# Writing out the last slots of a recurrent layer by hand, and moving three steps around its start

## The reference, cut to what matters

```python
# end of layer 2
h = _layer_norm(x, ln_mlp_scale, ln_mlp_offset)
x = x + jax.nn.gelu(h @ w_fc1 + b_fc1, approximate=False) @ w_fc2 + b_fc2
# layer 3
xa = _ln(x, ln1_w, ln1_b)
sx = jnp.concatenate([state[:, 1:2] - xa[:, :1], xa[:, :-1] - xa[:, 1:]], axis=1)
xxx = jnp.tanh((xa + sx * maa_x) @ maa_w1).reshape(b, l, 5, DM)
xxx = jnp.einsum('blfd,fde->blfe', xxx, maa_w2)
xm = xa[:, :, None] + sx[:, :, None] * (maa_stack + xxx)
xk, xw, xv, xr, xg = (xm[:, :, j] for j in range(5))
w = jnp.exp(-jnp.exp(time_decay + jnp.tanh(xw @ td_w1) @ td_w2))
r, k, v, g = xr @ Wr.T, xk @ Wk.T, xv @ Wv.T, _silu(xg @ Wg.T)
def step(s, rkvw):
    r_t, k_t, v_t, w_t = rkvw
    a = k_t[..., :, None] * v_t[..., None, :]
    out = jnp.einsum('bhi,bhij->bhj', r_t, u * a + s)
    return a + w_t[..., :, None] * s, out
# out, normed per head -> og
x1 = x + og * g @ Wo.T
xc = _ln(x1, ln2_w, ln2_b)
sx2 = jnp.concatenate([state[:, 0:1] - xc[:, :1], xc[:, :-1] - xc[:, 1:]], axis=1)
rr = jax.nn.sigmoid((xc + sx2 * ffn_maa_r) @ Wfr.T)
kk = jnp.square(jax.nn.relu((xc + sx2 * ffn_maa_k) @ Wfk.T))
return x1 + rr * (kk @ Wfv.T)
```

## Time and profile before

| | |
|---|---|
| median of 3 timed runs | 1012.68 us |
| the three runs | 1005.13, 1012.68, 1013.59 us |
| the profiled execution: its time | 1015.81 us |
| the profiled execution: its span | 1014.0 us |
| PE busy | 956.1 us (94% of the span) |
| DVE, ACT, POOL busy | 596.8, 451.3, 411.4 us |
| mean granted clock of TensorE | 0.983 of 2.4 GHz |

### The profile page before, as it was taken

The page is one execution under the profiler, slowest core; times in us unless marked ns, Lnnn a source line. Parts: engine busy times, 40 slices in busy tenths (PEclk is TensorE's granted clock), DMA queues, the critical chain, the costliest instruction groups (busy, mean ns, idle before and its releaser), DMA issues.

```text
span 1014.0 us, 21415 instructions
## 1 busy us (share of the span) xinstructions
PE 956.1 (94%) x8312; PEld 802.4 (79%) x8312; DVE 596.8 (59%) x972; ACT 451.3 (45%) x990; POOL 411.4 (41%) x572
## 2 busy tenths in 40 slices
PE   6999998988999999999999999999997999999986
PEld 4777776866789888899988998888996876778754
DVE  5999994767534444334464344443357648999851
ACT  3566763248543333333344333333323244666543
POOL 2243356875366234334156342343317722443320
PEclk9999999999999999999999999999999997999978
DMA  8100000310021111011101111110100100000000
GB/s 293 32 22 2 2 1 22 112 53 2 1 69 38 47 52 52 22 50 36 54 17 53 40 49 47 52 52 21 42 27 11 43 1 1 2 7 6 13 6 16
DMA packets 24146, 37.13 MB, mean 37 GB/s; under 512 B 4432, under 2 KB 16528, under 8 KB 23824
## 3 DMA queue, kind: packets, MB, share of 16 engines
q1 hardware_dynamic: 24080, 36.23, 11.4%
HBM read 35.17 MB, written 1.05 MB: 36 GB/s over the span
## 4 chain that ended last, share of the span: by engine, by line
PE 71%; DVE 14%; issue 5%; ACT 5%; POOL 4%; DMA 1%; DVEq 0%; ACTq 0%; POOLq 0%; SPq 0%
PE ps L1252 17%; PE ps L757 12%; PE ps L1269 9%; PE ps L1905 6%; PE ps L1311 6%; PE ps L1287 3%; PE ps L855 3%; DVE sb L634 2%; PE ps L1297 2%; DVE sb L628 2%; PE ps L2058 1%; PE ps L1983 1%; DVE sb L2350 1%; ACT sb L1692 1%; PE ps L269 1%
## 5 line engine op out<-in xcount | busy, mean ns | idle before, releaser
L804 POOL TENSOR_TENSOR sb<-sb 128x256 fp32r<-128x256 f32 (+1 forms) x128 | 101.4, 792 | 286.0 <-DMA sb<-in_heads_a 151.5
L1252 PE MATMUL ps<-sb 128*128 128x512 f32 x768 | 187.8, 396 | 1.0 <-issue 1.0
L1252 PEld LDWEIGHTS ps<-sb 128*128 128x128 f32 x768 | 139.5, 188 | 33.0 <-ACT sb L1385 3.1
L757 PE MATMUL ps<-sb 128*128 128x256 f32 x1152 | 149.0, 286 | 1.2 <-DVE sb L901 1.1
L757 PEld LDWEIGHTS ps<-sb 128*128 128x128 f32 x1152 | 141.4, 191 | 4.5 <-issue 2.6
L806 POOL TENSOR_TENSOR sb<-sb 128x256 fp32r<-128x256 f32 (+1 forms) x128 | 116.7, 912 | 10.1
L1482 DVE SCALAR_TENSOR_TENSOR sb<-ps,sb 128x512 fp32r<-128x512 f32 x64 | 45.1, 746 | 96.3 <-ACT sb L1418 96.3
L1269 PE MATMUL ps<-sb 128*128 128x256 f32 x768 | 99.2, 285 | 0.4 <-DVE sb L1450 0.4
L1269 PEld LDWEIGHTS ps<-sb 128*128 128x128 f32 x768 | 95.0, 191 | 3.0 <-issue 0.9
L1462 DVE TENSOR_REDUCE sb<-ps 128x8 f32<-128x520 f32 x32 | 22.4, 700 | 126.6 <-PE ps L1287 126.6
L1905 PE MATMUL ps<-sb 128*128 128x128 f32 (+2 forms) x576 | 87.7, 308 | 9.3 <-ACT sb L2208 6.4
(11 more groups left out here) (215 smaller groups left out, 1660.5 us busy)
## 6 DMA issues: line engine op xcount, KB each, us to landing
sb<-in_heads_a SPq DMA_DIRECT2D x32, 386.0 KB, 3.0
sb<-in_heads_c SPq DMA_DIRECT2D x16, 256.0 KB, 3.7
sb<-in_heads_b SPq DMA_DIRECT2D x32, 128.0 KB, 3.0
sb<-in_mlp_a SPq DMA_DIRECT2D x16, 128.5 KB, 2.1
sb<-in_mlp_b SPq DMA_DIRECT2D x16, 128.0 KB, 2.0
sb<-in_w_r SPq DMA_DIRECT2D x1, 2048.0 KB, 7.6
sb<-in_encT SPq DMA_DIRECT2D x1, 1024.0 KB, 7.3
sb<-in_ctx SPq DMA_DIRECT2D x1, 1024.0 KB, 7.1
```

The costliest lines, as they stand in the source:

```text
L757: last = pe.matmul(m.acc(t), lhsT[x], rhs[w], start=opens and n == 0, stop=False, skip_group_check=True)
L804: pool.tensor_tensor(high, src, one, ALU.mult).then_inc(*G.did(name + "_high", u))
L1252: last = pe.matmul(m.ps[u][:, c, :], m.w_parts[u][w][:, (KD * q + k) * P:(KD * q + k + 1) * P], rows[x][:, k, c * 512:(c + 1) * 512], star ...
```

## The change

`add_row_gpsimd` for `b_fc2` goes behind the splits of round 1. On PE, `fc1` of the last block (second half, round 3) goes ahead of the first tile's `turn`; on DVE, the split of its result goes from ahead of slot 0 into slot 3, behind tile 0's `shift` and `lora_rows`. In slot 5 on DVE, `gate` goes ahead of `receive`; on PE, two `warm` matmuls go ahead of the wait for that gate. PE's and ACT's loops end after slot 8 and DVE's after slot 11; what was left of tiles 3 to 7 is written out step by step. In it the keys and the receptance of tiles 5 and 7 (`APART`) get PSUM banks of their own, `ffn1` is cut in two (`ffn_keys`, with a signal of its own, and `ffn_receive`), `ffn2` of tiles 5 and 7 no longer waits for the receptance, three groups of `warm(m.td_ps, 3)` are added, and a one-column activation, `table`, fetches the ACT table at a chosen place. ACT's `receive` gets a wait for `rf` of the tile before.

```diff
@@ -1868,6 +1866,8 @@
+LAST = TILES - 1
+APART = (LAST - 2, LAST)
@@ -1987,8 +1987,8 @@
-        if i == 3:
-            warm(m.ps[0][:, 0, :], 4)
+        if i in (1, 3):
+            warm(m.ps[0][:, 0, :], i + 1)
@@ -2038,40 +2038,49 @@
-        if i >= 1:
-            pe.wait_ge(*done["rf"].at(i - 1))
+        if i == APART[0]:
+            pe.wait_ge(*done["mixed"].at(LAST))
+        elif i >= 1:
+            pe.wait_ge(*done["rf"].at(i - 2 if i > APART[0] else i - 1))
         for k in range(KD):
-            last = pe.transpose(m.c1[:, k * P:(k + 1) * P], m.xn_last[i % 2][:, k * P:(k + 1) * P], m.ident[:, :])
+            last = pe.transpose(m.key_bank(i)[:, k * P:(k + 1) * P], m.xn_last[i % 2][:, k * P:(k + 1) * P], m.ident[:, :])
...
-    @of_tile
-    def ffn1(i):
+    ffn_parts = [(m.wr[:, W_FK, :, :], m.wr[:, W_FR, :, :], k, 1) for k in range(KD)]\
+        + [(m.wfks, m.wfrs, k, 0) for k in range(KD)]
+    @of_tile
+    def ffn_keys(i):
...
-        parts = [(m.wr[:, W_FK, :, :], m.wr[:, W_FR, :, :], k, 1) for k in range(KD)]\
-            + [(m.wfks, m.wfrs, k, 0) for k in range(KD)]
         for e in range(KD):
-            product(m.c1[:, e * P:(e + 1) * P], [(wk[:, k, e * P:(e + 1) * P], m.xc[:, k, :, s:s + S])
-                                                 for wk, _, k, s in parts])
-        for n, (_, wr, k, s) in enumerate(parts):
+            last = product(m.key_bank(i)[:, e * P:(e + 1) * P],
+                           [(wk[:, k, e * P:(e + 1) * P], m.xc[:, k, :, s:s + S]) for wk, _, k, s in ffn_parts])
+        last.then_inc(*done["kk_raw"].did(i))
+    @of_tile
+    def ffn_receive(i):
+        for n, (_, wr, k, s) in enumerate(ffn_parts):
             for b in range(2):
-                last = pe.matmul(m.c1[b * S:(b + 1) * S, D:2 * D], m.xc[:, k, b, s:s + S], wr[:, k, :], start=n == 0,
-                                 stop=n == len(parts) - 1)
+                last = pe.matmul(m.receive_bank(i)[b * S:(b + 1) * S, D:2 * D], m.xc[:, k, b, s:s + S], wr[:, k, :],
+                                 start=n == 0, stop=n == len(ffn_parts) - 1)
...
-        pe.wait_ge(*done["rr"].at(i))
-        product(m.c1[:, 0:D], [(m.kk[:, k * P:(k + 1) * P], m.wr[:, W_FV, k, :]) for k in range(KD)])\
+        if i not in APART:
+            pe.wait_ge(*done["rr"].at(i))
+        product(m.key_bank(i)[:, 0:D], [(m.kk[:, k * P:(k + 1) * P], m.wr[:, W_FV, k, :]) for k in range(KD)])\
...
-    fc1(pe, ph, m, rows_split, 0, 1, 3)
-    for slot in range(TILE_SLOTS):
+    for u in range(STREAMS):
+        fc1(pe, ph, m, rows_split, u, 1, 3)
+    for slot in range(LAST + 2):
@@ -2079,13 +2088,13 @@
-            fc1(pe, ph, m, rows_split, 1, 1, 3)
...
-        ffn1(slot - 5)
+        ffn_keys(slot - 5)
+        ffn_receive(slot - 5)
@@ -2101,6 +2110,34 @@
+    gather(LAST - 1)
+    decay2(LAST)
+    spread1(LAST)
+    center(LAST - 1)
+    ffn_keys(LAST - 3)
+    ffn_receive(LAST - 3)
+    turn_ffn(LAST - 2)
+    turn_heads(LAST - 1)
+    ffn2(LAST - 3)
+    warm(m.td_ps, 3)
+    attended(LAST - 1)
+    ffn_keys(LAST - 2)
+    gather(LAST)
+    warm(m.td_ps, 3)
+    center(LAST)
+    turn_ffn(LAST - 1)
+    ffn_receive(LAST - 2)
+    turn_heads(LAST)
+    ffn2(LAST - 2)
+    warm(m.td_ps, 3)
+    attended(LAST)
+    ffn_keys(LAST - 1)
+    ffn_receive(LAST - 1)
+    turn_ffn(LAST)
+    ffn2(LAST - 1)
+    ffn_keys(LAST)
+    ffn_receive(LAST)
+    ffn2(LAST)
@@ -2188,24 +2225,30 @@
         for k in range(KD):
-            last = act.activation(m.xc[:, k, :, 1:S + 1], m.c1[:, k * P:(k + 1) * P].rearrange("p (b s) -> p b s", b=2),
-                                  ACT.Identity, bias=m.col("r2_b", k), scale=m.col("r2_w", k))
+            last = act.activation(m.xc[:, k, :, 1:S + 1],
+                                  m.key_bank(i)[:, k * P:(k + 1) * P].rearrange("p (b s) -> p b s", b=2), ACT.Identity, bias=m.col("r2_b", k), scale=m.col("r2_w", k))
...
     def relu(i):
-        act.wait_ge(*done["kk_rr"].at(i))
-        act.activation(m.kr[:, :], m.c1[:, 0:D], ACT.Relu).then_inc(*m.own_act.did("relu", i))
+        act.wait_ge(*done["kk_raw" if i in APART else "kk_rr"].at(i))
+        act.activation(m.kr[:, :], m.key_bank(i)[:, 0:D], ACT.Relu).then_inc(*m.own_act.did("relu", i))
...
-        act.activation(m.thf[:, :], m.c1[:, D:2 * D], ACT.Tanh, scale=0.5).then_inc(*done["rr"].did(i))
+        if i >= 1:
+            act.wait_ge(*done["rf"].at(i - 1))
+        act.activation(m.thf[:, :], m.receive_bank(i)[:, D:2 * D], ACT.Tanh, scale=0.5).then_inc(*done["rr"].did(i))
...
+    def table(function):
+        act.activation(m.th[:, 0:1], m.col("eps"), function)
@@ -2272,6 +2315,42 @@
+    heads(LAST - 2)
+    gate(LAST)
+    project(LAST)
+    decay1(LAST)
+    ffn_rows(LAST - 3)
+    f_stats(LAST - 2)
+    decay2(LAST)
+    f_normed(LAST - 2)
+    square(LAST - 1)
+    std(LAST - 1)
+    table(ACT.Tanh)
+    relu(LAST - 3)
+    relu_square(LAST - 3)
+    heads(LAST - 1)
+    ffn_rows(LAST - 2)
+    receive(LAST - 3)
+    f_stats(LAST - 1)
+    relu(LAST - 2)
+    relu_square(LAST - 2)
+    f_normed(LAST - 1)
+    table(ACT.Sqrt)
+    square(LAST)
+    std(LAST)
+    table(ACT.Tanh)
+    heads(LAST)
+    ffn_rows(LAST - 1)
+    receive(LAST - 2)
+    f_stats(LAST)
+    f_normed(LAST)
+    relu(LAST - 1)
+    receive(LAST - 1)
+    relu_square(LAST - 1)
+    ffn_rows(LAST)
+    relu(LAST)
+    relu_square(LAST)
+    receive(LAST)
@@ -2425,10 +2504,9 @@
-    for r in (2, 3):
-        for u in range(STREAMS):
-            mlp_split(vec, ph, m, u, 1, r)
-    for slot in range(TILE_SLOTS):
+    for u, r in ((0, 2), (1, 2), (0, 3)):
+        mlp_split(vec, ph, m, u, 1, r)
+    for slot in range(LAST + 5):
@@ -2440,16 +2518,43 @@
+        if slot == 3:
+            mlp_split(vec, ph, m, 1, 1, 3)
...
+        if slot == 5:
+            gate(slot - 4)
...
-        gate(slot - 4)
+        if slot != 5:
+            gate(slot - 4)
...
+    products0(LAST)
+    bonus(LAST - 1)
+    out_heads(LAST - 1)
+    products1(LAST)
+    group_sum(LAST - 1)
+    scan0(LAST)
+    group_rstd(LAST - 1)
+    group_norm(LAST - 1)
+    scan1(LAST)
+    attended(LAST - 1)
+    receive(LAST)
+    ffn(LAST - 3)
+    close(LAST - 3)
+    bonus(LAST)
+    out_heads(LAST)
+    group_sum(LAST)
+    group_rstd(LAST)
+    group_norm(LAST)
+    attended(LAST)
+    for i in (LAST - 2, LAST - 1, LAST):
+        ffn(i)
+        close(i)
@@ -2684,6 +2789,8 @@
+        m.key_bank = lambda i: m.ps[1][:, 0, :] if i in APART else m.c1
+        m.receive_bank = lambda i: m.ps[1][:, 1, :] if i in APART else m.c1
@@ -2717,6 +2824,7 @@
+        m.tile_done["kk_raw"] = Signal(m.done["ctx_ps"].sem, len(ITEMS))
@@ -2810,8 +2918,11 @@
+            for sem, value in free[3]["wv"]:
+                pool.wait_ge(sem, value)
+            mlp_gpsimd(pool, ph["mlp2"], m, 20, (1,), False)
...
-            mlp_gpsimd(pool, ph["mlp2"], m, 20, False, free[3]["wv"])
+            mlp_gpsimd(pool, ph["mlp2"], m, 20, (2, 3), False)
```

More of the change, by code:

```diff
@@ L911, in mlp_vector, with mlp_gpsimd @@
             context_norm_vector(vec, m, r)
-def mlp_gpsimd(pool, ph, m, loads, first, before):
-    for sem, value in before:
-        pool.wait_ge(sem, value)
-    for r in range(1, MLP_ROUNDS):
+def mlp_gpsimd(pool, ph, m, loads, rounds, first):
+    for r in rounds:
         split_fc1(pool, ph, m, loads, r)
@@ L2410, in ffn @@
             vec.wait_ge(*done["out"].at(i - 1))
-        vec.scalar_tensor_tensor(out=m.rf[:, :], in0=m.thf[:, :], scalar=1.0, in1=m.c1[:, 0:D], op0=ALU.add,
+        vec.scalar_tensor_tensor(out=m.rf[:, :], in0=m.thf[:, :], scalar=1.0, in1=m.key_bank(i)[:, 0:D], op0=ALU.add,
                                  op1=ALU.mult).then_inc(*done["rf"].did(i))
@@ L2793, in _ @@
             attn0_gpsimd(pool, ph["mlp0"], m)
-            mlp_gpsimd(pool, ph["mlp0"], m, 0, True, [])
+            mlp_gpsimd(pool, ph["mlp0"], m, 0, range(1, MLP_ROUNDS), True)
             inorm_gpsimd(pool, heads[1], m, free[1])
```

## The result

The changed kernel takes 997.46 us in the median (995.07 to 1000.22), the kernel before took 1011.45 (1005.13 to 1013.59, one execution more than stood above); the ratio is 0.9867, with an interval of 0.9828 to 0.9906, so that the change makes the kernel 0.9 to 1.7% faster. The profiled execution took 1000.22 us with a span of 998.4, against 1015.81 and 1014.0. So 14.0 us went in the median and 15.6 in the profile, where 19.6 had been forecast.

A forecast was written before the change was run, and what follows sets the result against it. PE was taken to bound most of the kernel, with clock falls behind its waits and tile 7's hand-overs at the end. 1.1 + 5.5 + 13.0 + 0 = 19.6 us off 1012.68 gave 993.1 us, range 988 to 999.

The forecast's parts named there:

- the signs named as right: Clock 1.00 at tile 1's gate, prompt gate, earlier lora, POOL waits moved, tile 7's x1 some 11 us before the last store.
- the signs named as wrong: Long half clock in either place, PE idle behind a table load, MLP 2 us sooner, or tile 7's x1 barely sooner.
- The bias row, 0 us: In the last MLP, moving the row leaves POOL's sum unchanged, so PE's wait only shifts; 0, bounds 2.3 gained, 1 lost.
- Rival 3: In the last MLP, the bias row's move pays in full; 990.8 us, chance 0.04.
- The start, 1.1 us: Ahead of tile 0, moving the last block's fc1 and split brings lora 1.1 us sooner; bounds 0 and 1.5.
- The gate, 5.5 us: At tile 1's gate, removing PE's wait and the clock fall gains 5.5 us, carried on; bounds 1.9 and 6.8.
- rival 2: At tile 1's gate, the clock still falls, giving 1.9 instead of 5.5 us; 996.7 us, chance 0.11.
- The end, 13.0 us: In the written-out last tiles, the new order gains 14.4 us, taken as 13.0; bounds 8.5 and 14.4.
- the half fall that was allowed for: At PE's wait ahead of tile 4's ffn2, a short clock fall costing about 2.5 us, put at one half.
- Rival 1: At PE's wait for tile 4's receptance, clock low to about 984; end gives 8.5, total 997.6 us, chance 0.14.
- rival 4: At ACT's table loads in the end, drains take 2.8 us more; 995.9 us, chance 0.03.
- Rival 5: The written-out end runs at half clock throughout, losing 8.6 us there; 1014.7 us, chance 0.04.

The follow-up runs named there:

- undo_row: The changed kernel with the bias row ahead of round 1's splits on POOL again; 996.9 us, 0.986 of the time before.
- row_late: The changed kernel with the bias row behind the split of the last fc1 weights on POOL; 998.8 us (of 3), 0.984 of the time before.
- no_tables: The changed kernel without the three one-column activations that fetch ACT tables early; 999.9 us, 0.988 of the time before.
- undo_gate: The changed kernel with tile 1's gate behind receive on DVE again, without the two warm matmuls ahead of it; 1000.8 us, 0.989 of the time before.
- banks_only: The changed kernel with loops to slot 16 in the old order, keeping own PSUM banks and shorter waits; 1002.4 us, 0.989 of the time before.
- no_warm: The changed kernel without the nine warm matmuls of the written-out end; 995.7 us, 0.982 of the time before.
- undo_start: The changed kernel with the last block's fc1 behind tile 0's turn and its split ahead of slot 0 again; 1000.5 us, 0.989 of the time before.
- recv_first: The changed kernel with ACT's tanh of tile 4's receptance ahead of heads and ffn_rows; 997.9 us, 0.984 of the time before.
- undo_end: The changed kernel with loops to slot 16 again, without written-out end, own banks, table fetches or warm matmuls there; 1010.1 us, 0.997 of the time before.
- gate_both: The changed kernel with tile 2's gate ahead of receive too and three warm matmuls ahead of it; 994.3 us, 0.980 of the time before.

## Why the prediction was right, and where it was off

The time lies inside the range and the direction is as forecast; the value was 4.4 us too low. In the profile 4.0 us are missing, and two misses are in them: the gate brought 5.4 us less than its term and the end 1.4 us more. That the second hid a part of the first is luck. Of the signs named as right all came (clock, gate, `lora`, waits for POOL, though with an MLP 0.7 us longer, `x1` of tile 7 11.0 us ahead of the end of the last `close`), and of the signs named as wrong none came at the two places named; the long fall stood at a third place that no sign watched.

- *The bias row, 0 us:* right, and by its reason, that POOL's sum of work holds PE. It measured -0.7 in the profile. What the sum did not have is that the wait in the middle can bring a short fall of the clock, which is most of it. Rival 3 is refuted by `undo_row`, and `row_late` shows what it takes: the row has to leave the sum ahead of the last `fc1` split.
- *The start, 1.1 us:* 1.6 in its place (10.35 to 8.74 us), less the 0.6 by which the MLP ends later, is about the 1.1 of the profile at tile 0's `mix1`.
- *The gate, 5.5 us:* tile 3's `mix1` came 6.4 us sooner, 5.3 beyond the start's 1.1. The chain of DVE steps that was followed through the slot was right to 0.2 us. The step that failed is the next sentence, "it is carried on". DVE without waits means that PE has them: in a slot where DVE is the bound, PE waited 1.10 us for the next gate, and a fall of the clock took 5.2 us back (119.8 us in the middle against 114.6 in `undo_row` and `no_tables`, where the same wait was followed by none). Nothing of the 5.5 was carried on in the profiled execution. The text looked for falls where PE had waited in the old profile, and rival 2 put the fall at the same gate, not at the one behind. Its time, 996.7, is near what came. By the mean clocks two of the four executions had the fall, so the median holds about half of that loss; only one of them was profiled.
- *The end, 13.0 us:* 14.4 in the profile, which is the sum of the steps to 0.1 us, without the half fall that was allowed for. `x1` of tile 6 was put at 975.8 on the old clock and came 6.08 + 0.42 us behind tile 6's norm, 975.7; `x1` of tile 7 at 986.4, 986.45 measured; the end at 997.5, 997.5 measured. That `ffn2` of tile 4 would win nothing was right (2.10 us of waiting, 2.12 before), and so was the price if the clock falls there, in kind: 1.5 us (`undo_gate`, `undo_row`), not 2.5. Rival 1's long fall was in no version with the new order. What the text had wrong is the share: it gave the order all of it, and `banks_only` shows that the banks and their shorter waits carry 7.7 of the 14.3.
- *Table loads:* rival 4 did not come. A tanh is 0.02 us behind its load of 1.28 in the version without fetches, so that the drain that the Trainium skill (ScalarE: Activation LUTs, "What ACT_TABLE_LOAD costs") adds, about 1.38 us, is not seen, neither as idle time on either side of the load (in the changed kernel ACT ends at 965.43, loads from 965.45 to 966.73 and goes on at 966.75) nor in the end of 28.3 us.
- *Rival 5,* half clock throughout, was in no version with the new order.
- *Profile and median:* taking 3.1 us off for the distance between profile and median was sound, as the profile of the changed kernel was 2.8 us above its median again.

## What to carry to other kernels

When a wait goes, ask which engine is the bound of the stretch behind it and where the other ones will now wait; in a kernel like this one, where falls of the clock stood behind PE waits of 1 to 2 us, a gain is safe only when the next wait is covered too, and one profile can't price an edit of under 1%. A step that is moved within the list of a full engine wins nothing until it leaves the part of the list that somebody waits for. For the last tiles of a pipeline, follow one tile by hand from engine to engine, and count own buffers and shorter waits as gains apart from the order.

## What was not expected of the hardware

The same wait of PE, 1.09 or 1.10 us for tile 2's gate, stands in nine of the profiles, and what followed it differs: no fall in two (`undo_row`, `no_tables`), half clock for 3.4 us in two (`no_warm`, `banks_only`), for 10.2 us in two (`undo_start`, `recv_first`) and for 13.6 us in three (changed, `undo_end`, `row_late`). The middle took 114.6, 116.0, 118.3 and 119.8 us with them, so that the long fall costs 5.2 us. It need not begin at the wait: in `undo_start` PE works again from 868.72, and the clock falls at 870.9.

In the written-out end PE waits 2.10 us ahead of tile 4's `ffn2`. Four profiles have no fall there (changed, `undo_start`, `gate_both`, `row_late`), and `undo_gate` and `undo_row` have one of 3.4 us, as has `no_warm`. In the old order 2.12 us of waiting at the same place were followed by 13.6 us in two profiles and by 10.2 in `banks_only`. No run parts what decides between them. The wait for the gate stands beside matmuls on half and a quarter of the rows, the one in the end mostly beside matmuls on all rows, and that may be a part of it.

Executions of one kernel differ by this: of the 13 of the kernel before that ran beside the first four kernels, those with a mean clock of 0.993 and 0.976 took 1007.1 and 1019.6 us. The four executions of `gate_both`, which leaves PE no wait at tile 2's gate, vary by 2.2 us.
